# The nine small places of the last stage stand in front of its last four large places

## The reference

```python
gate_logits = jnp.einsum('td,ed->te', xf, gate_w)
gate_scores = jax.nn.sigmoid(gate_logits + balance_bias)
topk_scores, topk_idx = jax.lax.top_k(gate_scores, ACTIVE_EXPERTS)          # 2 of 8
topk_scores = topk_scores / (topk_scores.sum(axis=-1, keepdims=True) + 1e-06)
comb = comb.at[jnp.arange(T)[:, None], topk_idx].add(topk_scores)
h = jax.nn.silu(jnp.einsum('td,ehd->teh', xf, w1))                          # 256 -> 512
expert_out = jnp.einsum('teh,edh->ted', h, w2)                              # 512 -> 256
out = jnp.einsum('te,ted->td', comb, expert_out)
x = x + out
```

## Time and profile before

| | |
|---|---|
| median of 3 runs | 3186.55 us (3186.21 to 3189.1) |
| span of the profiled execution, first to last instruction | 3192.7 us |
| time of the profiled execution outside its span | not recorded apart |
| busy in the span: TensorE, VectorE, ScalarE, GpSimd | 85%, 60%, 48%, 47% |
| last stage: first row load issued | 2898.11 us |
| last stage: last scatter issued | 3186.15 us |
| last stage: scatters, weight loads, row loads | 71, 40, 40 |
| mean granted TensorE clock | 0.948 of full speed |

### The profile page before, as it was taken

How to read it: one execution, slowest core, us unless ns; L and a number is a source line. 1 busy time by engine, 2 the same in 40 slices (tenths; PEclk the granted TensorE clock), 3 DMA queues, 4 the chain that set the end, 5 groups by cost and what they waited for, 6 DMA issues and landing times.

```text
span 3192.7 us, 49458 instructions
## 1 busy us (share of the span) xinstructions
PE 2706.0 (85%) x16590; PEld 1843.1 (58%) x16590; DVE 1901.0 (60%) x3490; ACT 1523.4 (48%) x2639; POOL 1499.6 (47%) x1618
## 2 busy tenths in 40 slices
PE   6888888876888788878999999899888888866997
PEld 2333333324655466644688887697555555545886
DVE  3788888884888578863222222402789999862111
ACT  4656666643776466631122221443666666641332
POOL 3577776663444477634322222200355555543443
PEclk8999999998999899989999999899999999978999
DMA  9700000000005000002377775100000000005785
GB/s 323 235 1 1 0 1 1 1 1 29 16 13 186 14 1 0 1 22 88 112 214 208 214 206 147 58 1 1 8 25 32 28 29 32 25 21 168 219 217 168
DMA packets 137955, 244.73 MB, mean 77 GB/s; under 512 B 15936, under 2 KB 111424, under 8 KB 127040
## 3 DMA queue, kind: packets, MB, share of 16 engines
q1 hardware_dynamic: 111168, 207.61, 20.0%
q0 software_dynamic: 26592, 34.63, 5.7%
HBM read 151.28 MB, written 92.73 MB: 76 GB/s over the span
## 4 chain that ended last, share of the span: by engine, by line
PE 35%; DVE 7%; POOL 5%; issue 5%; ACT 2%; DMA 1%; POOLq 0%; SPq 0%; DVEq 0%; ACTq 0%
PE PS L2261 11%; PE PS L2217 6%; PE PS L1886 4%; PE PS L2519 4%; PE PS L2506 4%; POOL e_hs L1445 2%; DVE e_mx L1348 1%; POOL e_qs L1448 1%; POOL rows_in_place L866 1%; PE PS L1300 1%; PE PS L1877 1%; DVE e_pr L1352 1%; DVE e_den L1359 1%; PE PS L1291 1%; DMA out<-f_y,f_token 1%
## 5 line engine op out<-in xcount | busy, mean ns | idle before, releaser
L566 POOL TENSOR_TENSOR u_in<-dtx,b_rep 128x512 f32<-128x512 f32 x256 | 325.4, 1294 | 200.8 <-ACT b_rep L547 199.7
L582 DVE TENSOR_TENSOR_SCAN state<-PS,u_in 128x512 f32<-128x512 f32 x256 | 312.4, 1220 | 59.3 <-POOL u_in L566 35.0
L539 PE MATMUL PS<-scaled,ident 128*128 128x512 f32 x512 | 295.8, 662 | 28.1 <-DVE scaled L576 28.0
L2278 ACT ACTIVATE d_act_b<-PS 128x256 f32<-128x256 f32 (+2 forms) x192 | 76.6, 400 | 443.4 <-PE PS L2261 406.3
L1445 POOL TENSOR_TENSOR e_hs<-e_pr 128x512 f32<-128x512 f32 x128 | 163.0, 1273 | 228.4 <-ACT e_pr L1412 226.5
L2261 PE MATMUL PS<-d_unit_T,d_w 128*128 128x256 f32 (+1 forms) x1280 | 260.6, 356 | 1.1 <-ACT d_unit_T L2271 1.1
L2287 DVE TENSOR_TENSOR d_hid<-d_act_b,PS 128x256 f32<-128x256 f32 (+2 forms) x192 | 84.5, 441 | 281.0 <-ACT d_act_b L2278 249.3
L2181 POOL DMA_INDIRECT out_by_token<-d_y_rows,d_token x71 | 110.3, 1553 | 300.8 <-DVE d_y_rows L2308 206.4
L555 ACT ACTIVATE PS<-dt,decay_rate 128x508 f32<-128x508 f32 x256 | 173.5, 687 | 138.2 <-DVE state L582 136.6
L2261 PEld LDWEIGHTS PS<-d_unit_T,d_w 128*128 128x128 f32 x1280 | 221.0, 190 | 26.4 <-DVE d_hid L2287 1.3
L576 DVE TENSOR_TENSOR scaled<-state,PS 128x512 f32<-128x512 f32 x256 | 169.5, 665 | 55.5 <-PE PS L520 43.8
(11 more groups left out here) (459 smaller groups left out, 6298.7 us busy)
## 6 DMA issues: line engine op xcount, KB each, us to landing
d_w<-in_d_w SPq DMA_DIRECT2D x42, 1024.0 KB, 5.7
f_w<-in_f_w SPq DMA_DIRECT2D x40, 1024.0 KB
rows_in_place<-blank SPq DMA_DIRECT2D x136, 272.0 KB, 4.9
d_w<-in_d_w SPq DMA_DIRECT2D x42, 512.0 KB
rows_by_expert<-zeros SPq DMA_DIRECT2D x36, 272.0 KB, 3.6
d_unit_rows<-rows_by_expert SPq DMA_DIRECT2D x31, 272.0 KB
f_unit_rows<-rows_in_place SPq DMA_DIRECT2D x31, 272.0 KB
X<-in_x SPq DMA_DIRECT2D x8, 512.0 KB, 11.8
```

What stands on the lines that cost most here:

```text
L539: nc.tensor.matmul(YB[:, c], ident[:], scaled[:, (KD * n + c) % RC], start=False, stop=n == NS - 1).then_inc(m_y, 1)
L566: nc.gpsimd.tensor_tensor(u_in[:, k % RU], dtx[:, p, c], b_rep[:, n % RB], ALU.mult).then_inc(m_u, 1)
L582: nc.vector.tensor_tensor_scan(state[:, k % 2], DECAY[:, k % RD], u_in[:, k % RU], 0.0, ALU.mult, ALU.add).then_inc(m_h, 1)
```

## The change

The small places, which stood behind all large ones, now stand before the last four large ones. The places themselves keep their tile numbers, and so their rows and experts.

```diff
 def unit_plan(groups):
 
     full, single = split_units(groups)
-    return [(2, 2 * n) for n in range(full)] + [(1, 2 * full + n) for n in range(single)]
+    pairs = [(2, 2 * n) for n in range(full)]
+    return pairs[:-4] + [(1, 2 * full + n) for n in range(single)] + pairs[-4:]
```

## The result

The changed kernel is slower: median 3201.09 us (20 runs) against 3188.28 us for the kernel before (20 runs beside them), a ratio of 1.0043 with a 95% interval of 1.003 to 1.0055. That is 13.7 us of 3188.28, with an interval of 9.6 to 17.5. The forecast was 3184.2, with 3190.5 as its upper end. The profiled execution took 3204.72 us with a span of 3202.9.

The account below looks back on a forecast made before the run. The prediction took the last stage's chain of serial scatters to end last: large places at chain speed give 4.9 us, loads beside small scatters take 2.5 back, so -2.4 off the 3186.55 us median gave 3184.2, range 3179.5 to 3190.5.

Parts of the forecast that it names:

- What bounds the stage: Last stage: TensorE paces the large places, but the chain of serial scatters ends last, 14.2 us after TensorE's last f_y starts.
- a sign of being wrong: TensorE's end in the last stage: a move by more than the chain's 8 us of cover would show the prediction wrong.
- L26 to S0: Scatter chain, from the large place now ahead of the small ones to the first small place: 7.58 us, bounded below by 6.50.
- S0 to S8: Scatter chain across the nine small places: 39.31 us as before, plus 2.5 for weight loads now beside the late ones.
- Back-pressure: Four f_y buffers and token copies in the last stage: no stall reaches TensorE, or it lies under the chain's 8 us.
- L27: First large place behind the small ones: its scatter starts 8 us behind its second f_y.
- S8 to L27: Scatter chain, from the last small place to the first large one behind it: 3.60 us, an empty place's interval.
- L27, L28, L29: Scatter intervals of three large places behind the small ones: 6.45 us each, 19.35 in all, at the chain's own speed.
- The sum: Last stage's scatter chain added up: last landing at 3186.55 against 3188.91, a change of -2.4 us.
- late small scatters queue behind the weight loads as S1 did: Rival, the last five small places: 3.5 us more per scatter, +12.5 us in all, 3199.1 us; chance 0.04.
- the rival with 2.1 us for each landing beside a load: Rival, five late small scatters: each lands 2.1 us later beside a load, +5.6 us in all, 3192.2 us; chance 0.08.
- the estimate by the Trainium skill's page "DMA: Bandwidth & Descriptors": Five late small scatters: 1.8 us more each from HBM access at high load, making the sum +4.1 us instead of -2.4.

Follow-up runs that it names:

- e14: The changed kernel run again, unedited, for a second profile: last stage 306.3 us, after 307.7 in the first.
- e3: The changed kernel with the empty last large place moved ahead of the small places and four filled large ones last: ratio 1.0041 to the kernel before.
- e10: The changed kernel, each weight load waiting until GpSimd has issued the scatters of the place five earlier: ratio 1.0006 to the kernel before.
- e13: The changed kernel with eight y and token buffers instead of four, and weight loads delayed as in e10: ratio 0.9996 to the kernel before.
- e15: The kernel before run again, unedited, for a second profile: last stage 292.3 us, after 290.8 in the first.
- e2: The changed kernel with the nine small places' weight loads cut to one eighth: ratio 0.9987 to the kernel before.
- e8: The changed order, but with the nine small places in front of the last large place alone: ratio 1.0023 to the kernel before.
- e4: Spread order, one small place behind each three large ones and the last four large ones at the end: 3250.93 us, ratio 1.0184 to the kernel before.
- e9: The spread order of e4, each weight load waiting until GpSimd has issued the scatters of the place five earlier: ratio 1.002 to the kernel before.
- e17: The changed kernel with SP issuing each place's weight load ahead of its row load: ratio 1.0012 to the kernel before.
- e1: The changed kernel with eight buffers for y and token instead of four: ratio 1.0017 to the kernel before.
- e7: The spread order of e4 with eight buffers for y and token instead of four: ratio 1.0025 to the kernel before.

## Why the prediction was wrong

- **What bounds the stage**: right. The chain of serial scatters ends last, and TensorE's last `f_y` (3177.09) stands 22 us ahead of the last landing, where I had 12 to 14. But TensorE's end moved too, which I had named as a sign of being wrong: this `f_y` starts 285.7 us into the stage, and 276.6 before.
- **L26 to S0**, 7.58 forecast: 11.87 measured, 9.46 in e14. I took the like of L30, which I had myself found to be empty; L26's second tile landed after 9.16 us. A mis-sized term of 2 to 4 us, for which 7.58 should have been a lower bound and not the value. e3 shows that it is not the cause of the rest, and with the lock gone it remains: 10.09 in e10, 11.39 in e13. It alone is enough to take up the -2.4 us that I forecast.
- **S0 to S8**, 39.31 + 2.5 forecast: 59.02 measured (3112.38 to 3171.40), 60.37 in e14. This is the step that failed. I priced contention scatter by scatter, as if loads fell at random beside them, and took most of it from the intervals that had got off lightly. The 7.94 us interval of S1, with a load 1.30 us behind its start, was the one row that showed the price; I weighed it as one in eight.
- **Back-pressure**, the reason behind it: "SP waits for the copies of three places before, also done. So no stall reaches TensorE; if one did, it would lie under the chain's 8 us." Wrong in each part. SP's row loads waited 29.2 us for held token copies, and with them the weight loads behind them; TensorE waited 9.8 us for weights. And it isn't hidden under the chain, since it sets the time at which the load meets the scatter, and so lengthens the chain itself. I had checked whether anything waits, not when the released things are sent off.
- **L27**, forecast to start 8 us behind its second `f_y`: 17.0. **S8 to L27**, 3.60: 3.59. **L27, L28, L29**, 6.45 each: 6.43, 6.53, 6.53. Right to 0.1 us.
- **The sum**: the misses of 4.3 (L26), 17.2 (S0 to S8), 0.1 (the large ones) and 0.5 (L26 starts 2.33 instead of 1.81 us behind its second `f_y`) make 22.1. From L26's second `f_y` (3107.78 before, 3098.18 after) to the last landing are 81.1 and 100.9 us, 19.8 more; -2.4 + 22.1 = 19.7. Up to that `f_y` the changed stage was 2.9 us quicker in these two profiles (206.8 against 209.7), which the edit does not explain; so the stages differ by 16.9, and by 14.0 in e14 and e15.
- **The rivals**: "late small scatters queue behind the weight loads as S1 did" gave 3199.1, and was right in sign and in price: S2 to S6 took 2.6 to 4.1 us more each than before, where it had 3.5. Its place was S4 to S8, two too late, and it had neither the ring nor L26's interval, so that its 12.5 us lie so near the measured 13.7 is in part luck. I gave it 0.04, on the ground that three of five were empty; but the empty S6 took 6.80 to land beside a load. That is 4.0 us over its 2.76, so the rival with 2.1 us for each landing beside a load fell short. So did the estimate by the Trainium skill's page "DMA: Bandwidth & Descriptors": its section "Latency and other measured facts" gives 0.2 and 2 us for access to HBM, on average and at high load, a difference of 1.8. The measurement decides.

What is shown: the lock recurs (e14), it needs full weight loads issued while the backlog stands (e2, and the last load of e8), it goes when the same loads come later, though the DMA engines are then busier (e4, e9, e10), and its link is SP's queue (e17, with e1 and e7 for the buffers). Two weight loads on top of each other are not it: in the lock they are issued 7.4 to 8.7 us apart, in e10 4.7 to 5.6 (S5's to L28's). Not shown is why a load at the same offset costs some scatters much more than others (S5 in e10, seven large places in e9), and what happens inside the DMA engines. In e4 the price of a load on a large scatter is 9.2 - 6.5 = 2.7 us. One load of 1.05 MB at 400 to 436 GB/s, as the busiest stretches of 2 us in the last stage of the kernel before reach, would take 2.4 to 2.6 us by my estimate; that fits a scatter that lets the whole load by. The Trainium skill's same page, section "SWDGE vs HWDGE vs iDMA", says that each DMA engine serves its internal queues in turn; how much of a load goes by in a turn no run here shows.

## What to carry to other kernels

In a serial chain of transfers, look at when the big transfers are issued against the chain's starts, not only at how full the engines are: here a load 1.2 to 1.6 us behind a start mostly went with an interval 2 to 4.5 us longer, and the same load at 3.75 us cost most of the large places little or nothing. Where the landing that starts the next link also frees a buffer that some queue waits for, the collision can repeat itself for as long as the backlog stands; more buffers, another order in the queue or a deliberately later issue breaks it. Before pricing a moved step from its neighbour's row, ask whether that neighbour did real work.

## What was unexpected of the hardware

The DMA engines were less busy in the lock (0.66 over 200 us in e4) than ahead of it (0.76), and than at the same time with the loads delayed (0.75 in e9). A scatter that moves no bytes still landed 4.0 us later beside a load (6.80 against 2.76). And delaying every weight load by a wait took the spread order from 1.0184 to 1.002.
